# One fused four-block kernel: all four groups of X rounded by VectorE, the last two behind the FFN's first and second tile

## The reference

```python
def fp4_quant_dequant(x):                 # blocks of 16 along the last dim
    xb = x.reshape(shape[:-1] + (shape[-1] // BLOCK, BLOCK))
    scale = jnp.maximum(jnp.max(jnp.abs(xb), axis=-1, keepdims=True) / 6.0, 1e-12)
    idx = jnp.searchsorted(_MID, jnp.abs(xb / scale))
    return (_GRID[idx] * jnp.sign(xb / scale) * scale).reshape(shape)
def fp4_linear(x, w):
    return jnp.einsum('bsk,nk->bsn', fp4_quant_dequant(x), fp4_quant_dequant(w))
h = silu(fp4_linear(x, w_gate)) * fp4_linear(x, w_up)     # 256 -> 704
return fp4_linear(h, w_down)                              # 704 -> 256
```

## Time and profile before

| | |
|---|---|
| runs, median (lowest to highest) | 1659.32 us (1657.69 to 1660.31), 3 runs |
| profiled execution, time | 1654.58 us |
| profiled execution, span | 1652.8 us |
| mean granted TensorE clock | 0.977 |
| TensorE busy | 1549.2 us (94%) |
| VectorE busy | 1294.7 us (78%) |
| ScalarE busy | 923.4 us (56%) |
| GpSimd busy | 288.9 us (17%) |

### The profile page before, as it was taken

The page is one execution under the profiler, slowest core; times in us unless marked ns, Lnnn a source line. Parts: engine busy times, 40 slices in busy tenths (PEclk is TensorE's granted clock), DMA queues, the critical chain, the costliest instruction groups (busy, mean ns, idle before and its releaser), DMA issues.

```text
span 1652.8 us, 29366 instructions
## 1 busy us (share of the span) xinstructions
PE 1549.2 (94%) x11202; PEld 991.8 (60%) x11202; DVE 1294.7 (78%) x2505; ACT 923.4 (56%) x1406; POOL 288.9 (17%) x383
## 2 busy tenths in 40 slices
PE   5977999999999999899999989999998999999986
PEld 2747899999853333785433378643336864333674
DVE  3585466553359998897999979799998979999596
ACT  1222344444137888444788844468885355888632
POOL 0063233221401120301111021111110210000030
PEclk8988999999989999999999999999999999999998
DMA  4125877776333220002421000232200022220000
GB/s 142 51 77 167 254 246 253 247 252 212 92 52 81 53 44 9 1 1 64 88 55 43 13 1 1 64 77 53 55 15 1 1 49 55 40 40 2 1 1 26
DMA packets 80310, 123.13 MB, mean 74 GB/s; under 512 B 13657, under 2 KB 55898, under 8 KB 80170
## 3 DMA queue, kind: packets, MB, share of 16 engines
q1 hardware_dynamic: 70794, 93.46, 21.5%
q0 software_dynamic: 9376, 27.80, 5.9%
HBM read 76.84 MB, written 18.61 MB: 58 GB/s over the span
## 4 chain that ended last, share of the span: by engine, by line
PE 73%; DVE 16%; ACT 5%; issue 3%; DMA 2%; POOL 1%; SPq 1%; DVEq 0%; POOLq 0%; ACTq 0%
PE PS L1116 15%; PE PS L1069 13%; PE PS L992 7%; PE PS L1102 7%; PE PS L980 6%; DVE MX L1656 6%; PE PS L1224 4%; PE PS L1234 4%; PE PS L1039 3%; PE PS L1053 2%; PE PS L925 2%; PE PS L1261 1%; PE PS L969 1%; DMA Pb<-W 1%; PE PS L1186 1%
## 5 line engine op out<-in xcount | busy, mean ns | idle before, releaser
L1656 DVE TENSOR_REDUCE MX<-PS 128x1 f32<-128x512 f32 x1024 | 635.4, 683 | 28.9 <-PE PS L1069 25.5
L774 ACT ACTIVATE Pb<-PS 128x1024 f32<-128x1024 f32 x512 | 519.4, 1026 | 124.7 <-PE PS L1102 124.7
L1069 PE MATMUL PS<-Ks,Qs 48*128 48x512 f32 x1024 | 386.6, 453 | 1.5 <-DVE MX L1656 0.9
L1102 PE MATMUL PS<-Qs,Ks 50*128 50x512 f32 x1024 | 360.0, 451 | 0.0
L1116 PE MATMUL PS<-Pb,V 128*32 128x256 f32 x4096 | 320.5, 390 | 0.5
L1069 PEld LDWEIGHTS PS<-Ks,Qs 48*128 48x128 f32 x1024 | 159.9, 184 | 203.7 <-DVE MX L1656 143.1
L1116 PEld LDWEIGHTS PS<-Pb,V 128*32 128x32 f32 x4096 | 83.9, 108 | 164.2 <-ACT Pb L774 112.8
L1102 PEld LDWEIGHTS PS<-Qs,Ks 50*128 50x128 f32 x1024 | 143.8, 185 | 24.0 <-ACT Pb L774 19.8
L992 PE MATMUL PS<-Pb,OT 128*128 128x256 f32 x624 | 141.0, 379 | 0.0
L980 PE MATMUL PS<-Ks,Qs 128*128 128x256 f32 x936 | 127.4, 294 | 7.2 <-DVE Ks L1528 7.2
L980 PEld LDWEIGHTS PS<-Ks,Qs 128*128 128x128 f32 x936 | 119.7, 197 | 9.7 <-DVE Ks L1528 8.6
(11 more groups left out here) (296 smaller groups left out, 2167.3 us busy)
## 6 DMA issues: line engine op xcount, KB each, us to landing
Pb<-W SPq DMA_DIRECT2D x78, 512.0 KB, 4.3
y_slot<-V SPq DMA_DIRECT2D x39, 256.0 KB, 4.0
Qs<-Qh SPq DMA_DIRECT2D x128, 64.0 KB, 2.3
Ks<-Kh SPq DMA_DIRECT2D x120, 64.0 KB, 2.3
V<-b SPq DMA_DIRECT2D x39, 128.0 KB, 3.7
XT<-x_mid POOLq DMA_DIRECT2D x4, 1024.0 KB, 6.5
out<-Pb POOLq DMA_DIRECT2D x4, 1024.0 KB, 6.7
OT<-xT SPq DMA_DIRECT2D x2, 1024.0 KB, 6.4
```

What stands on the lines that cost most here:

```text
L774: F["ex"].inc(act.activation(weights_of(n), PS[:, 2 * (n % 2):2 * (n % 2) + 2, :], ACT.Exp, scale=0.25))
L1069: F["slp"].inc(pe.matmul(PS[:, slot_bank(i), :], Qs[rows, p % NB, t * P:(t + 1) * P], Ks[rows, p % NB, kh * HALF:(kh + 1) * HALF], start=T ...
L1102: ins = pe.matmul(PS[:, 2 * (n % 2) + a, :], Ks[rows, p % NB, kt * P:(kt + 1) * P], Qs[rows, p % NB, qh * HALF:(qh + 1) * HALF], start=Tru ...
L1656: F["sld"].inc(dve.tensor_reduce(MX[:, p % 2, a, t, kh:kh + 1], PS[:, slot_bank(i), :], AX.X, ALU.max))
```

## The change

GpSimd's ten instructions and ScalarE's two absolute values for groups 2 and 3 go away, as do `maxima_x` and `scales_x`. VectorE calls `quant_x(2)` behind the rounding of the FFN's tile 0 and `quant_x(3)` behind that of tile 1. ScalarE's `magnitude` for them stands behind `silu(1)` and `silu(2)`. `hidden_turn(t)` numbers the turns of the shared semaphores `zq` and `am`, which now alternate between H and X for the first two tiles. TensorE waits for `xq` for all tiles of X.

```diff
@@ ScalarE
-                for k in range(2):
-                    F["px"].wait(act, b, k + 1)
-                    F["xm"].inc(act.activation(XM[k], XQ[:, (2 + k) * w:(3 + k) * w], ACT.Abs))
                 for t in range(TT - 1):
-                    magnitude(2 + t, qm_h, qn_h)
+                    magnitude(hidden_turn(t), qm_h, qn_h)
                     if t:
                         h_evac(t - 1)
                     silu(t + 1)
+                    if t < 2:
+                        magnitude(hidden_turn(t) + 1, XQ[:, (2 + t) * w:(3 + t) * w], XW[:, 0:w])
@@ TensorE, x_tile_turn
-                    if t < 4:
-                        F["xq"].wait(pe, b, t // 2 + 1)
-                    else:
-                        F["xp"].wait(pe, b, t // 2 - 1)
+                    F["xq"].wait(pe, b, t // 2 + 1)
@@ VectorE
-                quant_x(1, lambda: maxima_x(2))
-                scales_x(2)
-                maxima_x(3)
-                scales_x(3)
+                quant_x(1, lambda: None)
                 for t in range(TT):
...
-                    F["hq"].inc(round_blocks(b, 2 + t, Hb, I, h_b, HQ, qn_h, qm_h, link, meanwhile, room))
+                    F["hq"].inc(round_blocks(b, hidden_turn(t), Hb, I, h_b, HQ, qn_h, qm_h, link, meanwhile, room))
+                    if t < 2:
+                        quant_x(2 + t, lambda: None)
@@ GpSimd
-                for k in range(2):
-                    F["xr"].wait(pool, b, k + 1)
-                    F["px"].inc(pool.tensor_tensor(blocks(xq[k]), X[:, 4 + 2 * k:6 + 2 * k, :].rearrange("p t (k w) -> p (t k) w", w=BLK),
-                                                   spread(qin, 2 + k), ALU.mult))
-                for k in range(2):
-                    F["xm"].wait(pool, b, k + 1)
-                    F["px"].inc(pool.tensor_scalar(XM[k], XM[k], 1.0, STEP, ALU.max, ALU.mult))
...
-                    F["px"].inc(pool.tensor_tensor(xq[k], xq[k], XM[k], ALU.add))
...
-                    F["px"].inc(pool.tensor_tensor(xq[k], xq[k], XM[k], ALU.subtract))
...
-                    F["xp"].inc(pool.tensor_tensor(blocks(xq[k]), blocks(xq[k]), spread(qsc, 2 + k), ALU.mult))
```

More of the change, by code:

```diff
@@ L236, in transformer @@
         HT = Pf[1][:, 0:IC * P].rearrange("p (c n) -> p c n", c=IC)
-        XM = [XW[:, 2 * D:4 * D], OTf[:, 5 * I:5 * I + 2 * D]]
         qmx = sb("qmx", [P, TT * D // BLK])
@@ L277, in transformer @@
             op=TT // 2, on=TT, mp=TT, mt=TT, pr=TT, rr=TT,
-            xq=2, zq=2 + TT, am=2 + TT, xr=2, px=8, xm=2, xp=2, gup=TT, sg=TT, hh=TT, hq=TT, htp=TT, htv=TT, dp=TT, dr=TT,
+            xq=4, zq=4 + TT, am=4 + TT, gup=TT, sg=TT, hh=TT, hq=TT, htp=TT, htv=TT, dp=TT, dr=TT,
             outd=16, ahead=0, chain=0,
@@ L281, in transformer @@
         F = {k: Flow(sem("f_" + k), v) for k, v in flows.items()}
-        CHAIN, AHEAD = 82, 13
+        CHAIN, AHEAD = 86, 13
         F["ahead"].per = AHEAD
@@ L303, in slot_bank, with hidden_turn @@
             return (4, 5, 6, 0, 1, 2)[i % 6] if i < UN else 4 + (i - UN) % 3
+        def hidden_turn(t):
+            return 2 + t + min(t, 2)
         def weights_of(n):
@@ L574, in sequence @@
                             gather(TT + 2 * (u - UPPER) + n)
[L576 to L579, removed]
-                for k in range(2):
-                    F["xr"].wait(pool, b, k + 1)
-                    F["px"].inc(pool.tensor_tensor(blocks(xq[k]), X[:, 4 + 2 * k:6 + 2 * k, :].rearrange("p t (k w) -> p (t k) w", w=BLK),
-                                                   spread(qin, 2 + k), ALU.mult))
-                for k in range(2):
-                    F["xm"].wait(pool, b, k + 1)
-                    F["px"].inc(pool.tensor_scalar(XM[k], XM[k], 1.0, STEP, ALU.max, ALU.mult))
-                    F["px"].wait(pool, b, 2 + 3 * k + 1)
-                    F["px"].inc(pool.tensor_tensor(xq[k], xq[k], XM[k], ALU.add))
-                    F["px"].wait(pool, b, 2 + 3 * k + 2)
-                    F["px"].inc(pool.tensor_tensor(xq[k], xq[k], XM[k], ALU.subtract))
-                    F["px"].wait(pool, b, 2 + 3 * k + 3)
-                    F["xp"].inc(pool.tensor_tensor(blocks(xq[k]), blocks(xq[k]), spread(qsc, 2 + k), ALU.mult))
                 if more:
@@ L844, in sequence @@
                 h_evac(TT - 2)
-                magnitude(1 + TT, qm_h, qn_h)
+                magnitude(hidden_turn(TT - 1), qm_h, qn_h)
                 if more:
@@ L1722, in quant_x @@
                     block_scales(x_of(g), P, w, b_of(g), link)
-                    F["xq"].inc(round_blocks(b, g, x_of(g), w, b_of(g), XQ[:, g * w:(g + 1) * w], XW[:, 0:w], XQ[:, g * w:(g + 1) * w],
+                    F["xq"].inc(round_blocks(b, g if g < 2 else hidden_turn(g - 2) + 1, x_of(g), w, b_of(g), XQ[:, g * w:(g + 1) * w], XW[:, 0:w], XQ[:, g * w:(g + 1) * w],
                                              link, meanwhile))
[L1726 to L1736, removed]
                 def x_low(t):
```

## The result

The changed kernel took 1673.92 us in the median (1673.57 to 1678.72, 4 runs), the kernel before 1658.51 us (1657.33 to 1660.31, 4 runs). The ratio is 1.0098, 95% interval 1.0086 to 1.0110: 14 to 18 us slower. Forecast were +16.3 us, a median of 1676 us and 1671 to 1682.

The account below looks back on a forecast made before the run. VectorE was taken to bound each FFN stage up to tile 3, TensorE from down(2). Per sequence 9.54 added - 2.47 removed - 2.89 slowing = +4.18 us; over four sequences +16.3, so 1659.3 becomes 1675.6, said as 1676, range 1671 to 1682.

Parts of the forecast that it names:

- The handover: First sequence's FFN: VectorE bounds through tile 3, TensorE from down(2) at 719.69, after waiting 0.28 us for ScalarE's copy.
- Removed ahead of tile 0: VectorE, first scale to tile 0's product: 2.47 us gone; group 2's maxima lay in a wait and bring nothing.
- The slowing by GpSimd: VectorE's tiles 0 and 1 lose GpSimd's slowdown, 1.47 + 1.42 = 2.89 us; bounds 1.69 to 3.0.
- Added: VectorE ahead of tile 2's product: quant_x(2) and quant_x(3), 4.77 us each, 9.54 us together.
- The estimate of 3.8 us: Group 2 on VectorE by the skill's twice-as-fast rule: some 3.8 us instead of 4.77, each sequence 1.9 us less.
- Sum: VectorE by tile 2: 9.54 - 2.47 - 2.89 = +4.18 us; sequences 4.2 + 4.2 + 3.7 + 4.2 = +16.3 us.
- a rival at +0.5: TensorE's gate_up(3): low clock behind the second pause makes down(2) +0.5 us later each sequence; median 1678, chance 0.22.
- a sign of being wrong: TensorE: pauses not moving to before gate_up(2) and gate_up(3), or the clock staying low behind the second.
- rival 1: The second pause cools TensorE too: small form +0.5 us a sequence (0.22), large up to 2.6 (0.08); together 0.30.
- The pauses: TensorE waits 0.8 us for tile 0, about 4.5 us ahead of gate_up(2), 2.6 us ahead of gate_up(3).
- The range: Median 1671 to 1682 us, from the terms' bounds, a second cool stretch and about 2 us of spread.

Follow-up runs that it names:

- fill: The changed kernel with VectorE's waits for ScalarE filled by maxima, scales and next tiles' products, same instructions in another order: 1659.48 us, ratio 1.0012.
- warm2: The changed kernel with 15 identity matmuls on TensorE ahead of gate_up(2) and 12 ahead of gate_up(3): 1674.10 us, ratio 1.0096.
- relief: The kernel before without GpSimd's ten instructions and ScalarE's two absolute values, groups 2 and 3 of X left unrounded: 1646.54 us, ratio 0.9932.
- only2: The kernel before with group 2 of X alone moved to VectorE, behind tile 0's rounding; GpSimd still rounds group 3: 1677.89 us, ratio 1.0116.
- only2_warm: The kernel with group 2 alone on VectorE, plus 17 identity matmuls ahead of tile 0's transposes and 14 ahead of gate_up(2): 1671.97 us, ratio 1.0081.
- late: The kernel before, GpSimd keeping both groups, group 3 wholly behind group 2; VectorE's maxima and scales moved into its waits, ScalarE's absolute values later: 1653.14 us, ratio 0.9967.
- only3: The kernel before with group 3 of X alone moved to VectorE, behind tile 1's rounding; GpSimd still rounds group 2: 1666.85 us, ratio 1.0055.
- warm: The changed kernel with 32 identity matmuls on TensorE in each pause, ahead of gate_up(2) and of gate_up(3): 1690.84 us, ratio 1.0203.

## Why the prediction was right, point by point

- **The handover.** VectorE up to tile 3, TensorE behind it: right. In the first sequence down(2) still waits 0.27 us for ScalarE, and a delay of 4.08 us at tile 2 is one of 4.08 at down(2) and at down(7). fill moves both back, and warm2 shows that the low clock behind TensorE's pauses costs 1 us in all. In the fourth sequence TensorE decides in both kernels, as forecast.
- **Removed ahead of tile 0:** 2.47 us forecast, 2.54 measured. That group 2's maxima bring nothing was nearly right: they brought 0.07 us, since the wait there grew from 0.50 to 1.02 us.
- **The slowing by GpSimd:** 2.89 us forecast, 8.74 + 8.69 - 2 x 7.26 = 2.91 measured. relief shows its cause by taking GpSimd's work away, with two absolute values of ScalarE that ran before the slowed additions. Another 0.42 us of slowing lay in the scales ahead of tile 0; the prediction had it unseen inside the 2.47 us removed there, so its sum is right all the same.
- **Added:** 2 x 4.77 forecast, 4.77 + 4.76 measured. The rule of the Trainium skill, "GPSIMD Engine Reference", section "Key points", that the prediction weighed against this is one on elementwise work alone, and there VectorE was more than twice as fast: the five instructions took 7.7 us on GpSimd, and the four of the same task on VectorE 4 x 0.69 = 2.76. The estimate of 3.8 us set it against a whole group, which also has maxima, scale, reciprocal and a wait, so it was no measure of the 4.77.
- **Sum:** 9.53 - 2.54 - 2.91 = 4.08 against 4.18; over four sequences 16.85 against 16.3. By sequences it was 4.2, 4.2, 3.7, 4.2 forecast and 4.1, 4.5, 4.2, 4.1 measured. The half microsecond more in the second and third is the lower clock behind the second pause, which I had put in a rival at +0.5 and left out of the main sum. Without it the sum would be some 15.9 us. The prediction also named a clock that stays low behind the second pause as a sign of being wrong. By that sign it failed in two sequences of four: that pause is not harmless there, though the cost was the small one of rival 1 and stayed inside the range. That the total came so near is partly luck, since this term was missing and VectorE's sum was 0.1 us a sequence too high.
- **The pauses:** 4.5 and 2.6 us forecast, 4.47 and 2.20 measured in the first sequence; tile 0's came out at 1.21 instead of 0.8, mainly because gate_up(1) began 0.3 us earlier than counted (15.07 us from group 0's maxima instead of 15.38). The second pause was 1.62, 2.64 and 2.09 us in the other sequences.
- **The range** was held. The median that was forecast lies 2.1 us above the measured one: 0.8 because the kernel before measured lower this time, 0.4 from rounding up to 1676, 0.9 because the medians differ by 15.4 and not by 16.3.

In only2 the granted clock was 0.50 behind the pauses, in only2_warm, where they were mostly filled, 1.00. The rule of the Trainium skill, "TensorE: Matmul & The Clock Gate", section "What's actually happening", that the clock halves after idleness, agrees with this. What the low clock costs depends on who waits for gate_up(2): about 6 us in only2, where silu(2) came late for tile 2's product, and nothing in the changed kernel, where gate_up(2) was done in time at either clock.

## What to carry to other kernels

Price moved work by where it lies on the path, not by busy time: here 65 us less on GpSimd and 7 us more on VectorE made the kernel some 16 us slower, because each moved block also brought its wait for another engine onto the path, and some of the work that went had lain in a wait and freed nothing. Before taking work off a helper engine, try to put what the main engine does for it into waits that are there anyway (late, -5.5 us), and if it is moved, interleave it with the next tile's work (fill gave back some 90% of the loss). Work on GpSimd was not free for VectorE here: measure its share by leaving it out (relief, -11 us), for its slowing moves with it (late).

## What the runs showed of the hardware

- VectorE's two-input instructions on SBUF took up to 2.1 times as long beside GpSimd's elementwise work (0.89 to 1.84 us for 128x704), while its reductions (0.89 us at 698.36 in the kernel before) and the product with one operand in PSUM (0.88 us at 697.45) did not change. Short instructions were slowed too: one with one input from 0.17 to 0.59 us (687.60 in the kernel before), a 128x16 product from 0.17 to 0.58 us (714.54 in late).
- One GpSimd group slowed VectorE by 2.24 us when it lay on tile 0 alone (only3). Two of them slowed tiles 0 and 1 by 2.91 us in the kernel before, where part of them lay on reductions and waits.
- A pause of 2.20 or 2.09 us ahead of gate_up(3) left the clock at 2.4 GHz in two sequences, pauses of 1.62 and 2.64 us were followed by 1.2 GHz in the other two: in one program, the length of the pause did not tell which. In relief pauses of 2.35 us had the lower clock behind them in two sequences and the full one in the other two.
- The start of the first FFN stage varied from 671.0 to 678.4 us among ten profiled kernels that are alike up to there. Spans of single profiles do not resolve a change of a few microseconds; times counted from a point just ahead of the change do: tile 2's product lay at 37.00 to 37.03 us in all sequences of the changed kernel, warm and warm2.
